# Making the fourth layer's context keys and values in 24 units beside the first layer's chain

## The chip, the cores and the metric

One core of a Trainium2 chip runs one program. The metric is the device time of a run in microseconds. Three runs of the kernel before took 933.57, 928.25 and 932.36 us, median 932.36.

## What is computed

The reference is a four-layer stack of gated cross-attention and feed-forward blocks. `x` is 8 batches of 56 tokens, 128 wide; the context is 8 batches of 1500 rows, 128 wide. What matters here:

- Layer 0: attention to the context with normalised, positive key features, so that only sums over the context are needed (per batch a 128 x 128 matrix and a vector), then a feed-forward block with ternary weights and 8-bit activations.
- Layer 1: attention in a window over the first 56 context rows, then 16 experts.
- Layer 2: attention of latents to the layer-normed context. The keys' L2 norms over 8 heads of 64 are needed for every context row.
- Layer 3: attention of 16 heads to all 1500 context rows with keys `ctx @ Wk.T` and values `ctx @ Wv.T`, then 8 experts. The keys are needed as a 16-bit part and a 16-bit remainder.

What depends on the context alone can be made before `x` is known: layer 0's sums, layer 2's normed context and key norms, layer 3's keys and values.

## The kernel before, in words

Five engines run programs of their own, written out by hand and joined by semaphores; each runs its instructions strictly in the order written. SyncE (`sync`) issues all DMAs, also in order: a wait there holds back every later DMA.

**The context pass** (about 9 to 252 us) is one turn per batch b, with buffers p = b % 2. TensorE's `context` makes, from the turned context `cT[p]`: the centred context (L679, three banks "D", PSUM 3 to 5), layer 3's keys (L687, three uses of banks D), layer 0's keys and values (L696, six uses of banks "A", PSUM 0 to 2), `l0_sums` of the batch before (L658, banks 6 and 7), layer 3's values (L708, three uses of banks A), half of `l2_keys` of the batch before (L668, twelve 125 x 512 products in all, 16-bit), the transposes of the normed context (L721) and the other half. VectorE scales the centred context (L1698), takes the keys' remainders `k_lo` (an L1519 with a 16-bit result), makes `kpr` (L1664), the statistics of the next batch (L1678 on `c_in`), reduces the squares (L1717), makes `kn` (L1519, 125 x 1536), and sums the squares of `l2_keys` (`l2_norms`, L1670) around the remainder of `clnT`. ScalarE copies and squares (L1190 `k_hi`, L1196, L1198, L1211 and L1213 the values into `v3`, L1181 squares, L1222). GpSimd waits for `kn`, applies gain and bias (L1411, L1412) and makes `rhs0` from `c_in` (L1420), which ends the use of `c_in[p]`.

`bank_a` and `bank_d` are the cyclic uses of three banks each; `a_uses` counts those of A. In `store_results` SyncE stores per turn `cln`, three copies of the keys (`k_hi`, `k_lo`, `k_hi`, L489), the values (L491), loads `cT` and, after `l0_rhs`, `c_in` of batch b + 2 (L453), and stores `clnT`. Weights come in portions after turns 1 to 5, the broadcast `vec` with turn 3.

**After the pass** come the key norms of the last batch (12 tiles), then the chain of layer 0: a layernorm of `x` (each with a 4-element power on GpSimd, L1430), the products of L738 and L742 and the queries, the attention result `at0` (signalled by `l0_att`, VectorE after L785), its store to `d_att` and load back as `y2` (L530, L533), `quantised_weights` on VectorE (L1619 to L1626), the dense product, a layernorm and the first feed-forward block (`quantised_ffn`, eight hidden products into eight banks). Layer 1 follows: queries, `key_blocks` on GpSimd (L1444), `scores1`, and `shift1` on VectorE, whose first mask addition (L1519 into 128 x 1024) starts at 345 us. Beside the chain SyncE loads layer 1's and 2's weights and the first experts into `wex`.

Of the kernel before, what the change touches and what calls it, by code (L numbers as in the profile page):

```python
# [15 lines left out]
D = 128  # L16
# [99 lines left out]

PRODUCT = {"latent_q": 18, "latent_k": 22, "latent_qT": 23, "queries2": 24}
# [57 lines left out]

def a_uses(b):

    return 0 if isinstance(b, int) and b == 0 else 21 * b - 12


def build(nc, io, out):
    ctx = ExitStack()
    with ctx:
# [86 lines left out]
        clnT = [carve([D, 2, C], F16) for _ in range(2)]  # L270
# [5 lines left out]
        k_hi = [carve([D, C], F16) for _ in range(2)]  # L276
        k_lo = [carve([D, C], F16) for _ in range(2)]
        v3 = [carve([KP, KT, 192]) for _ in range(2)]
        sqk = carve([KP, SQ, I2])
        stat = carve([KP, KT, 6])  # L280
        sm = carve([KP, 16, 24])
        wraw = carve([D, 5, FF])
# [101 lines left out]
        w_ready = sem("weights_ready")  # L384
        c_var, c_sd = sem("context_variance"), sem("context_deviation")
# [64 lines left out]
        def _(sp):  # L450
# [31 lines left out]
            def store_results(b, p, more=True):  # L482

                sp.wait_ge(d_free, 9 * b + 3 + 3)
                sp.dma_start(batch(d_cln, b), cln[p].rearrange("p j d -> p (j d)")).then_inc(st[p], 16)

                sp.wait_ge(d_free, 9 * b + 3 + 6)
# [8 lines left out]
                sp.wait_ge(d_free, 9 * b + 3 + 9)  # L496
                sp.dma_start(batch(d_clnT, b), clnT[p]).then_inc(st[p], 16)

            portions = {1: rest[0:1], 2: rest[1:2], 3: rest[2:5], 4: rest[5:10], 5: rest[10:14]}
            for b in range(B):  # L500
                store_results(b, b % 2, more=b + 2 < B)
                for dst, src in portions.get(b, ()):
                    sp.dma_start(dst, src).then_inc(ld_w, 16)

            for p in range(2):
                sp.wait_ge(st[p], 96 * (B // 2 + 1))
# [11 lines left out]
            for dst, name in ((w_kT2, "L2_wkT"), (w_vT2, "L2_wvT"), (w_o2, "L2_wo"), (w_q2, "L2_wq"),  # L518
                              (qk_col, "qk_cols")):
                sp.dma_start(dst, io[name]).then_inc(ld_m, 16)  # L520

            def load_experts1(g, p):
                sp.dma_start(wex[p][:, 0:G1 * 3 * D], batch(io["L1_ex"], g)).then_inc(ex_ld[p], 16)

            load_experts1(0, 0)
            load_experts1(1, 1)


# [5 lines left out]
                .then_inc(l0_ld, 16)  # L534

# [48 lines left out]
            sp.wait_ge(l3_free, 1)  # L584
            for p in range(2):
# [39 lines left out]
        def _(pe):  # L625
# [21 lines left out]
            def bank_d(b, n):  # L647

                pe.wait_ge(d_free, 9 * b + n + 1)
                return 3 + n % 3  # L650

            def l0_sums(b, p):
# [3 lines left out]
                pe.wait_ge(acc_used, b + 1)  # L656
                for j in range(KT):
# [4 lines left out]
            def l2_keys(turn, p, first_use, tiles=range(KT)):  # L662

                pe.wait_ge(d_free, 9 * turn + 3)
                for j in tiles:
                    k = bank_a(turn, first_use + j)
# [5 lines left out]
            def context(b, p, loads, first=False):  # L672
# [12 lines left out]
                for u in range(3):  # L685
                    k = bank_d(b, 3 + u)
                    pe.matmul(ps[0:D, k, 0:4 * KP], w_k3,  # L687
                              cT[p][:, 4 * u:4 * u + 4, :].rearrange("p j n -> p (j n)"),
                              start=True, stop=True).then_inc(d_full, 1)

# [1530 lines left out]
```

## Time and profile before

| | |
|---|---|
| median of three runs | 932.36 us |
| the profiled execution's own time | 930.32 us |
| its span | 928.7 us |
| busy TensorE, VectorE, ScalarE, GpSimd | 743.2, 632.5, 397.1, 277.1 us |
| mean granted clock of TensorE | 0.861 of full |
| bytes moved by DMA | 93.98 MB, 101 GB/s over the span |
| context pass, to the memset ahead of the first layernorm | 253 us |
| from there to the first mask addition of layer 1 | 92 us |

The profile gives for one execution when each instruction began and how long it took, what ended the idle time ahead of it, and for a stretch the busy time of each engine, the clock granted to TensorE (1.00 is 2.4 GHz, 0.50 is 1.2 GHz), the busy share of the 16 DMA engines and what they moved. Instructions that begin one after another on one engine overlap a little, so a row's mean can exceed the distance to the next. A line such as L1519 is that of a helper and stands for many operations; they are told apart by shape.

### The profile page before, as it was taken

The page shows a single profiled execution, that of the slowest core. Times are in us where ns is not written, and L with a number is a line of the kernel's source. Part 1 is how long each engine was busy: PE and PEld are TensorE (multiplying, and loading weights), DVE is VectorE, ACT ScalarE, POOL GpSimd, SP SyncE. Part 2 cuts the span into 40 slices and gives each one's busy share as a digit, 9 for nine tenths or more (in the row PEclk, how much of TensorE's full clock was granted, in tenths as well). Part 3 has the DMA queues.
Part 4 walks back from the last instruction along what each step waited for, and adds up shares of the span by engine and source line. Part 5 has one row for each costly group of instructions (what it writes and reads, how often), then busy time and mean ns, then how long its engine had stood idle before and what let it go on. Part 6 is the DMA issues. An engine that isn't in the chain of part 4 may idle for free.

```text
span 928.7 us, 16098 instructions
## 1 busy us (share of the span) xinstructions
PE 743.2 (80%) x5460; PEld 491.3 (53%) x5460; DVE 632.5 (68%) x1302; ACT 397.1 (43%) x650; POOL 277.1 (30%) x215
## 2 busy tenths in 40 slices
PE   4879998899744357698589999993479999985996
PEld 3757776677532224566245555552226656653665
DVE  4879988897768847355655566557587998915653
ACT  1556656566500203154344544541006766752441
POOL 1441234423213011045147777770050000000111
PEclk9889999999965557599799999997558998996999
DMA  6467666564232000011502242205703445500230
GB/s 188 156 214 262 247 205 227 181 214 149 76 103 20 0 0 1 1 51 52 154 5 69 76 128 72 69 1 76 156 1 103 130 128 151 164 2 23 69 102 21
DMA packets 46648, 93.98 MB, mean 101 GB/s; under 512 B 16698, under 2 KB 30010, under 8 KB 44274
## 3 DMA queue, kind: packets, MB, share of 16 engines
q1 hardware_dynamic: 46594, 93.25, 34.5%
q8 instruction: 35, 0.57, 0.3%
q14 instruction: 19, 0.16, 0.1%
HBM read 61.58 MB, written 31.65 MB: 100 GB/s over the span
## 4 chain that ended last, share of the span: by engine, by line
PE 38%; DVE 23%; issue 4%; ACT 3%; POOL 3%; DVEq 0%; POOLq 0%; ACTq 0%
DVE arena L2067 8%; PE ps L972 7%; PE ps L962 6%; DVE arena L1519 5%; PE ps L907 3%; PE ps L1132 2%; PE ps L1142 2%; PE ps L1070 2%; PE ps L1059 2%; ACT arena L1350 1%; POOL arena L1489 1%; PE ps L920 1%; PE ps L1044 1%; PE ps L841 1%; POOL arena L1430 1%
## 5 line engine op out<-in xcount | busy, mean ns | idle before, releaser
L1519 DVE TENSOR_TENSOR arena<-ps,arena 128x448 f32<-128x448 f32 (+8 forms) x160 | 99.4, 642 | 66.8 <-ACT arena L1373 20.5
L2067 DVE TENSOR_REDUCE arena<-ps 112x1 f32<-112x500 f32 x192 | 115.5, 669 | 17.9 <-PE ps L1044 17.0
L1489 POOL TENSOR_TENSOR arena<-arena 125x448 f32<-125x448 f32 x96 | 108.8, 1133 | 24.5 <-ACT arena L1327 21.7
L1350 ACT ACTIVATE arena<-ps 125x896 f32<-125x896 f32 x96 | 87.0, 917 | 30.0 <-PE ps L1059 29.4
L1430 POOL TENSOR_TENSOR arena<-arena 112x4 f32<-112x4 f32 x11 | 11.3, 1024 | 292.8 <-DVE arena L1543 286.8
L972 PE MATMUL ps<-arena 125*128 125x448 f32 (+1 forms) x208 | 97.1, 548 | 1.3 <-ACT arena L1327 0.8
L1519 DVE TENSOR_TENSOR arena<-ps,rn 125x448 f32<-125x448 f32 x96 | 59.3, 618 | 50.0 <-PE ps L962 45.7
L1327 ACT ACTIVATE arena<-arena,kbias 125x448 f32<-125x448 f32 x96 | 63.7, 668 | 65.0 <-DVE arena L1519 46.3
L962 PE MATMUL ps<-arena 128*125 128x448 f16 (+3 forms) x312 | 78.0, 360 | 3.0 <-DVEq L1530 3.0
L668 PE MATMUL ps<-w_k2h,arena 128*125 128x512 f16 x288 | 69.0, 397 | 12.4 <-ACT arena L1213 12.2
L1411 POOL TENSOR_TENSOR arena<-arena,vec 125x1536 f32<-125x1536 f32 x8 | 27.6, 3455 | 152.9 <-DVE arena L1519 152.9
L962 PEld LDWEIGHTS ps<-arena 128*125 128x125 f16 (+1 forms) x312 | 40.8, 135 | 57.2 <-issue 42.3
L1670 DVE TENSOR_REDUCE rn<-arena 125x512 f32 (+1 forms) x96 | 60.9, 682 | 4.7 <-ACT arena L1181 4.7
L1181 ACT ACTIVATE arena<-ps 125x512 f32<-125x512 f32 x96 | 57.3, 597 | 15.4 <-PE ps L668 11.4
L1464 POOL TENSOR_TENSOR arena<-arena 112x512 f32<-112x512 f32 x26 | 32.9, 1266 | 99.8 <-DVE arena L1519 99.4
L1044 PE MATMUL ps<-arena 64*112 64x500 f16 x192 | 55.5, 452 | 7.1 <-issue 4.3
L668 PEld LDWEIGHTS ps<-w_k2h,arena 128*125 128x125 f16 x288 | 40.4, 143 | 36.4 <-ACT arena L1213 13.4
L1070 PE MATMUL ps<-arena 125*32 125x168 f32 x768 | 51.5, 342 | 8.4 <-ACT arena L1350 8.4
L972 PEld LDWEIGHTS ps<-arena 125*128 125x128 f32 (+1 forms) x208 | 37.8, 189 | 13.9 <-issue 8.4
L1132 PE MATMUL ps<-arena 128*128 128x448 f16 x192 | 41.4, 367 | 3.1 <-DVE arena L1519 3.0
L1059 PE MATMUL ps<-arena 64*125 64x112 f16 x768 | 43.8, 242 | 0.0
L696 PE MATMUL ps<-w_l,arena 128*125 128x256 f32 x192 | 43.0, 381 | 0.0
(276 smaller groups left out, 1361.9 us busy)
## 6 DMA issues: line engine op xcount, KB each, us to landing
d_k<-arena SPq DMA_DIRECT2D x24, 375.0 KB
d_v<-arena SPq DMA_DIRECT2D x8, 1125.0 KB
arena<-d_k SPq DMA_DIRECT2D x96, 93.8 KB
arena<-d_v SPq DMA_DIRECT2D x8, 1008.0 KB
arena<-in_ctxT SPq DMA_DIRECT2D x8, 750.0 KB, 13.6
d_cln<-arena SPq DMA_DIRECT2D x8, 750.0 KB
d_clnT<-arena SPq DMA_DIRECT2D x8, 750.0 KB
arena<-d_clnT SPq DMA_DIRECT2D x8, 750.0 KB
```

The costliest lines, as they stand in the source:

```text
L668: mm = pe.matmul(ps[0:KP, k, :], clnT[p][:, a, KP * j:KP * j + KP], w_k2h[:, w, :], start=(n == 0), stop=(n == 2))
L962: mm = pe.matmul(ps[0:rows, (t + p) % 2, 0:N].rearrange("p (h q) -> p h q", h=H8), clnT_s[p][:, a, cols:cols + rows], qtT[:, q, :, bass.ds ...
L972: pe.matmul(ps[0:D, 4 + 2 * p, 0:N], cln_s[p][0:rows, t, :], pexp[(t + p) % 2][0:rows], start=(t == 0), stop=(t == KT)).then_inc(l2_pv, 1)
L1044: pe.matmul(ps[0:TT, max_bank(bn, u), 0:500], q.rearrange("p o h q -> p (o h q)"), kst[pn][64 * r:64 * r + 64, g, 500 * third:500 * third ...
L1059: mm = pe.matmul(ps[0:KP, 2 * (t % 2) + r, 112 * g:112 * g + 112], kst[p][rows, g, KP * t:KP * t + KP], qst3[rows, b:b + 1, g, 2 * r:2 * r ...
L1070: pe.matmul(ps[32 * g:32 * g + 32, 6, 0:168], v3s[p][:, t, 32 * g:32 * g + 32], p3[t % 2][:, 3 * g:3 * g + 3, :].rearrange("p h q -> p (h ...
L1327: act.activation(pexp[(t + p) % 2][0:rows], sscl[(t + p) % 2][0:rows], ACT.Exp, bias=bias)\
L1350: act.activation(p3[t % 2].rearrange("p (k h) q -> p k (h q)", k=2), ps[0:KP, 2 * (t % 2):2 * (t % 2) + 2, 0:8 * S], ACT.Exp).then_inc(l3_ ...
L1489: ins = pool.tensor_tensor(psum2[p][0:rows], psum2[p][0:rows], pexp[(t + p) % 2][0:rows], ALU.add)
L1519: return dve.tensor_tensor(out, a, b, op)
L1670: dve.tensor_reduce(rn[:, bass.ds(turn - 1, 1), j, :].rearrange("p o h -> p (o h)"), sqk[:, j % SQ, :].rearrange("p (h d) -> p h d", h=H8) ...
L2067: dve.tensor_reduce(mx3[bn % 2][:, u % 2, u % 8 // 2, u // 8:u // 8 + 1], ps[0:TT, max_bank_of(bn, u), 0:500], AX.X, ALU.max).then_inc(l3_ ...
```

## The change

Layer 3's keys and values leave the context pass and are made in 24 units of a third of a batch (500 columns). A unit is one 128 x 500 key product into bank 6 and four 125 x 128 value products into bank 7 (TensorE, `later`), two copies of the keys (16-bit and 32-bit) and two of the values (ScalarE, `later`), the key remainder (GpSimd, `remainders`), and four stores (SyncE, `store_later`). Its results lie in two sets of buffers, `late_hi`, `late_k`, `late_lo`, `late_v`, by the unit's parity; ScalarE waits with unit u until the four stores of unit u - 2 have landed (`st_l`). Units 0 to 2 are batch 0 and run in its turn; 3 to 8 are batches 7 and 6, whose `cT` is still there; the others read `cT` reloaded into `wex` (`load_later`). The units stand at fixed places of each program, in groups.

The key norms of the last batch move from the end of the pass to behind `l0_att`, in banks 3 to 5. `quantised_weights` moves from VectorE to GpSimd; VectorE keeps the scales. The load of `cT` in `store_results` waits for the `w_l0` products. The first feed-forward block uses six banks for its hidden products, and both blocks two in place of four for the turned hidden tiles. Layer 2's weights and the first experts are loaded later, and SyncE and VectorE wait for all 24 units, VectorE ahead of `shift1(0)`.

```diff
@@ store_results, SyncE
-                for s, part in enumerate((k_hi[p], k_lo[p], k_hi[p])):
-                    sp.dma_start(k3_in[bass.ds(b, 1), s].rearrange("o h d c -> (o h) d c"), part).then_inc(st[p], 16)
-                sp.wait_ge(a_free, a_uses(b) + 3 + 9)
-                sp.dma_start(batch(d_v3, b), v3[p].rearrange("p j d -> p (j d)")).then_inc(st[p], 16)
+                if b == 0:
+                    for u in range(3):
+                        store_later(u)
                 if more:
+                    sp.wait_ge(a_full, a_uses(b) + 6)
                     load_turned(b + 2, p)
                     sp.wait_ge(l0_rhs, b + 1)
                     load_context(b + 2, p)
...
+            def load_later(i):
+                sp.dma_start(wex[i % 2][:, 0:C], io["ctxT"][LATER[3 + i]]).then_inc(ld_x[i % 2], 16)
+
+            def store_later(u):
+                b, at, h = LATER[u // 3], 500 * (u % 3), u % 2
+                sp.wait_ge(l_lo, u + 1)
+                for n, part in enumerate((late_hi[h], late_lo[h], late_hi[h])):
+                    sp.dma_start(k3_in[b:b + 1, n, :, :, at:at + 500].rearrange("o h d c -> (o h) d c"), part)\
+                        .then_inc(st_l[h], 16)
+                sp.wait_ge(lv_taken, u + 1)
+                sp.dma_start(batch(d_v3, b)[:, 768 * (u % 3):768 * (u % 3) + 768],
+                             late_v[h].rearrange("p j d -> p (j d)")).then_inc(st_l[h], 16)
...
+            for u in range(3, 9):
+                store_later(u)
 
             sp.wait_ge(l0_att, 1)
...
+            for u in range(9, 24):
+                store_later(u)
+                if u in (11, 14, 17):
+                    sp.wait_ge(lv_full, u + 1)
+                    load_later(u // 3 - 1)
...
@@ TensorE
+            def later(*units):
+                for u in units:
+                    i, third = u // 3 - 3, u % 3
...
+                    if u:
+                        pe.wait_ge(lk_taken, u)
+                    pe.matmul(ps[0:D, 6, 0:4 * KP], w_k3, tiles.rearrange("p j n -> p (j n)"),
+                              start=True, stop=True).then_inc(lk_full, 1)
+                    if u:
+                        pe.wait_ge(lv_taken, u)
+                    for j in range(4):
+                        mm = pe.matmul(ps[0:KP, 7, D * j:D * j + D], tiles[:, j, :], w_v3, start=True, stop=True)
+                    mm.then_inc(lv_full, 1)
...
-                for u in range(3):
-                    k = bank_d(b, 3 + u)
-                    pe.matmul(ps[0:D, k, 0:4 * KP], w_k3,
...
-            l2_keys(B, 1, 0)
...
+            later(3, 4)
+            later(5, 6)
+            later(7, 8)
...
+            later(9, 10)
+            pe.wait_ge(l0_att, 1)
+            l2_keys(B, 1, 0, bank=3)
+            pe.wait_ge(a_free, a_uses(B) + 3 + KT)
             pe.wait_ge(l0_ld, 16)
             transposes(y2, 4)
+            later(11)
...
+            later(12, 13, 14, 15, 16)
+                    later(17, 18)
+            later(19, 20, 21)
@@ ScalarE
+            def later(*units):
+                for u in units:
+                    h = u % 2
+                    if u >= 2:
+                        act.wait_ge(st_l[h], 64 * (u // 2))
+                    act.wait_ge(lk_full, u + 1)
+                    act.copy(late_hi[h], ps[0:D, 6, 0:500])
+                    act.copy(late_k[h], ps[0:D, 6, 0:500]).then_inc(lk_taken, 1)
+                    act.wait_ge(lv_full, u + 1)
...
+            later(7, 8, 9, 10)
+            l2_squares(B, 0, bank=3)
+            later(11)
...
+            later(12, 13, 14, 15, 16)
             for t in range(NT):
                 act.wait_ge(h_in[0], t + 1)
...
+            later(17, 18, 19, 20, 21, 22, 23)
@@ GpSimd
+            def remainders(*units):
+                for u in units:
+                    pool.wait_ge(lk_taken, u + 1)
+                    pool.tensor_tensor(late_lo[u % 2], late_k[u % 2], late_hi[u % 2], ALU.subtract).then_inc(l_lo, 1)
...
+            remainders(9, 10)
+            quantised_weights()
+            remainders(11)
+            rsqrt()
+            remainders(12)
+            rsqrt()
+            remainders(13, 14, 15, 16)
             pool.wait_ge(l1_k, 1)
             key_blocks(0)
+            remainders(17, 18)
             key_blocks(1)
+            remainders(19)
             rsqrt()
+            remainders(20, 21, 22, 23)
@@ VectorE
-            quantised_weights()
+            weight_scales()
+            l2_norms(B, 0)
...
+            for p in range(2):
+                dve.wait_ge(st_l[p], 64 * 12)
             shift1(0)
```

## Rows read from the trace of the kernel before

**Rows 1.** Windows: us, busy us and count of each engine, clock, DMA share, GB/s.

```profile
96.00:120.00 24.00, 23.32 (x141) 18.35 (x140) 22.21 (x54) 15.26 (x35) 7.66 (x5) 1.00 0.75 265
...
288.00:312.00 24.00, 6.84 (x48) 4.41 (x48) 20.03 (x51) 2.52 (x3) 7.36 (x5) 0.50 0.15 15
```

**Rows 2.** Timeline of VectorE in the pass: start us, duration us, instruction.

```profile
32.83 1.75 DVE L1519 TENSOR_TENSOR arena<-arena 125x1536 f32<-125x1536 f32 x1
...
87.05 1.75 DVE L1519 TENSOR_TENSOR arena<-arena 125x1536 f32<-125x1536 f32 x1
...
113.29 1.75 DVE L1519 TENSOR_TENSOR arena<-arena 125x1536 f32<-125x1536 f32 x1
...
127.88 0.67 DVE L1519 TENSOR_TENSOR arena<-ps,arena 128x500 f16<-128x500 f32 x1
...
130.36 0.95 DVE L1664 TENSOR_SCALAR arena<-arena 125x1536 f32<-125x1536 f32 x1
134.63 2.42 DVE L1678 BATCH_NORM_STATS2 arena<-arena 125x6 f32<-125x128 f32 x12 [3.32 <-DMA arena<-in_ctx]
...
142.33 1.75 DVE L1519 TENSOR_TENSOR arena<-arena 125x1536 f32<-125x1536 f32 x1
...
226.20 1.75 DVE L1519 TENSOR_TENSOR arena<-arena 125x1536 f32<-125x1536 f32 x1
...
243.12 0.29 DVE L1659 COPY kv_all<-ps 128x130 f32<-128x130 f32 x1 [4.33 <-PE ps L658]
```

**Rows 3.** Timeline of VectorE and SyncE behind the pass.

```profile
253.21 0.09 DVE L1760 MEMSET arena<- 128x32 f32 x1
...
284.54 0.34 SPq L530 DMA_DIRECT2D d_att<-arena  x1
...
286.58 7.58 DVE L1622 TENSOR_SCALAR arena<-arena,wscale 128x512 f32<-128x512 f32 x5
...
291.92 0.33 SPq L533 DMA_DIRECT2D arena<-d_att  x1
...
345.03 1.23 DVE L1519 TENSOR_TENSOR arena<-ps,cst 128x1024 f32<-128x1024 f32 x1 [3.80 <-PE ps L841]
```

**Rows 4.** Timeline of TensorE in the pass, the moved products.

```profile
125.95 3.17 PE L687 MATMUL ps<-arena,w_k 128*128 128x500 f32 x6 [0.76 <-DVE arena L1698]
...
136.82 2.78 PE L708 MATMUL ps<-w_v,arena 128*125 128x128 f32 x24
```

**Rows 5.** Instructions by line and shape: busy us, mean ns, idle before.

```profile
L1190 ACT CAST arena<-ps 128x500 f16<-128x500 f32 x24 | 13.8, 575 | 38.8 <-PE ps L687 38.8
...
L1211 ACT COPY arena<-ps 125x384 f32<-125x384 f32 x24 | 11.7, 489 | 0.0
...
L1464 POOL TENSOR_TENSOR arena<-arena 112x512 f32<-112x512 f32 x26 | 32.9, 1266 | 99.8 <-DVE arena L1519 99.4 <-POOL arena L1464 0.4
...
L1433 POOL MEMSET arena<- 128x1152 f32 x1 | 1.1, 1057 | 0.0
```

**Rows 6.** Timeline, the first reload of the context and its reader.

```profile
44.63 0.33 SPq L453 DMA_DIRECT2D arena<-in_ctx  x1
...
50.58 2.42 DVE L1678 BATCH_NORM_STATS2 arena<-arena 125x6 f32<-125x128 f32 x12 [5.17 <-DMA arena<-in_ctx]
```

**Rows 7.** DMA issues: operation, count, KB each, median us to landing.

```profile
wex<-in_L_ex SPq DMA_DIRECT2D x6, 576.0 KB, 3.9
...
d_rl<-arena SPq DMA_DIRECT2D x1, 14.0 KB, 1.7
```

**Rows 8.** Timeline of SyncE's queue: issues in groups, us for the whole group.

```profile
104.13 1.83 SPq L489 DMA_DIRECT2D d_k<-arena  x3
...
217.16 3.88 SPq L489 DMA_DIRECT2D d_k<-arena  x3
...
636.17 4.94 SPq L576 DMA_DIRECT2D arena<-d_k  x12
```

**Rows 9.** Windows of one us while one value store is under way.

```profile
231.00:232.00 1.00, 1.00 (x10) 0.88 (x9) 1.00 (x3) 1.00 (x4) 0.92 (x2) 1.00 0.33 138
```

More of the change, by code:

```diff
@@ L275, in build @@
         rhs0 = carve([KP, KT, D + 2])
[L276 to L279, printed above, removed]
         stat = carve([KP, KT, 6])
         sm = carve([KP, 16, 24])
+        at[0] = CTX_TOP
+        clnT0 = carve([D, 2, C], F16)
+        at[0] = LATE_AT
+        late_hi = [carve([D, 500], F16) for _ in range(2)]
+        late_lo = [carve([D, 500], F16) for _ in range(2)]
+        late_k = [carve([D, 500]) for _ in range(2)]
+        late_v = [carve([KP, 4, 192]) for _ in range(2)]
+        clnT = [clnT0, carve([D, 2, C], F16)]
+        at[0] = SQK_AT
+        sqk = carve([KP, SQ, I2])
+        at[0] = 32520
         wraw = carve([D, 5, FF])
@@ L384, in build @@
         w_ready = sem("weights_ready")
+        lk_full, lk_taken = sem("later_keys_full"), sem("later_keys_taken")
+        lv_full, lv_taken = sem("later_values_full"), sem("later_values_taken")
+        l_lo = sem("later_keys_remainders")
+        h_used = sem("first_hidden_banks_used")
+        w_scales = sem("weight_scales_ready")
+        ld_x = [sem(f"later_context_loaded{i}") for i in range(2)]
+        st_l = [sem(f"later_results_stored{i}") for i in range(2)]
         c_var, c_sd = sem("context_variance"), sem("context_deviation")
@@ L660, in l0_sums, with l2_keys @@
                 mm.then_inc(acc_full, 1)
-            def l2_keys(turn, p, first_use, tiles=range(KT)):
-                pe.wait_ge(d_free, 9 * turn + 3)
+            def l2_keys(turn, p, first_use, tiles=range(KT), bank=0):
+                pe.wait_ge(d_free, 6 * turn + 3)
                 for j in tiles:
-                    k = bank_a(turn, first_use + j)
+                    k = bank + bank_a(turn, first_use + j)
                     for n, (a, w) in enumerate(((0, 0), (0, 1), (1, 0))):
@@ L703, in context @@
                     l0_sums(b - 1, 1 - p)
-                for u in range(3):
-                    k = bank_a(b, 6 + u)
-                    for j in range(4):
-                        mm = pe.matmul(ps[0:KP, k, D * j:D * j + D], cT[p][:, 4 * u + j, :], w_v3,
-                                       start=True, stop=True)
-                    mm.then_inc(a_full, 1)
+                if first:
+                    later(0, 1, 2)
                 if first:
@@ L1185, in context @@
                     deviation(0)
-                act.wait_ge(st[p], 96 * loads)
-                for u in range(3):
-                    act.wait_ge(d_full, 9 * b + 3 + u + 1)
-                    act.copy(k_hi[p][:, 500 * u:500 * u + 500], ps[0:D, 3 + u, 0:500]).then_inc(k_hi_ready, 1)
                 act.wait_ge(l0_kn, b + 1)
@@ L1432, in _ @@
             rsqrt()
+            remainders(3, 4)
             ch.link(pool.memset(v1, 0.0))
@@ L1437, in _ @@
             pool.nop().then_inc(l1_zero, 1)
+            remainders(5, 6)
             rsqrt()
+            remainders(7, 8)
             def key_blocks(i):
@@ L1730, in context @@
                 if not first:
-                    l2_norms(b, 9, range(KT // 2))
+                    l2_norms(b, 6, range(KT // 2))
                 for u in range(3):
@@ L1874, in normalise1 @@
                 ins.then_inc(l1_on, 1)
+            for p in range(2):
+                dve.wait_ge(st_l[p], 64 * 12)
             shift1(0)
```

166 lines of the change are left out of this document (91 added, 75 removed).

## The prediction, made before the change was built

> **What bounds the kernel now.** I read the windows first, to see which stretch is full of what [rows 1]. Between 96 and 120 us TensorE is busy for 23.3 of 24 us and VectorE for 22.2: the context pass is short of engine time. Between 288 and 312 TensorE is busy for 6.8 us, at half clock, and ScalarE for 2.5: the first layer is a chain of small dependent steps, with room beside it. The change moves work from the first stretch to the second, and the question is what limits each afterwards.
>
> Next, the period of the pass. I mark a turn by T, the start of VectorE's multiply of 125x1536 that makes `kn` [rows 2]. T goes from 32.83 (batch 0) to 226.20 (batch 7), so seven turns take 193.4 us. An undisturbed one takes 26.2 (87.05 to 113.29), the next 29.0 (113.29 to 142.33) because the statistics wait 3.32 us for `in_ctx`. That wait closes a loop beside the engines: `kn` goes to GpSimd, whose three passes free `c_in`; only then is the next context load issued, 11.8 us after T (32.83 to 44.63 for batch 0 [rows 2, 6]); it lands after L; and from the start of the statistics to the next T there are 7.7 us (134.63 to 142.33). A turn can't be shorter than 19.5 + L.
>
> Third, the chain that follows it, from VectorE's memset at 253.21 to VectorE's first mask addition on the second layer's scores at 345.03 [rows 3]: 91.8 us, with the first layer's attention ready (`l0_att`) at 284.5, as the store of `d_att` shows.
>
> **The context pass.** Removed per turn: TensorE's 3.17 (keys) and 2.79 us (values) [rows 4]; VectorE's three remainders, 127.88 to 130.36, 2.5 us [rows 2]; ScalarE's 3 x 0.58 + 3 x 0.78 = 4.1 us [rows 5], the 0.78 being a 0.49 copy and its 128-wide sister of 0.29; 2250 KB of stores. VectorE's own path would then be 14.6 (T to the end of the norms and `cln`, 113.29 to 127.88), 0.95 for the key features and 7.7, so 23.2 us. But the loop is longer: L was 5.95 us where I can read it (issue 44.63, statistics 50.58) [rows 6], with the end of a value store still under way; the expert load of 576 KB lands in 3.9 us [rows 7], which in proportion is 5 for these 750 KB. I take L = 5.5 and 25.0 us a turn, bounds 24.4 and 25.5. So of about 3 us of VectorE work a turn only 1.2 come through.
>
> The start loses something. T of batch 0 comes at about 27.4 instead of 32.8, but units 0, 1 and 2 follow there with two buffers. Unit 0 is taken at 26.3, its remainder ends at 28.8, its stores are issued until 31 and land at 35.4; only then is unit 2 taken, and its remainder holds GpSimd until 37.9. GpSimd's passes (10.1 us) end at 48.0 against 44.6 before, and T of batch 1 is 48.0 + 5.5 + 7.7 = 61.2 (58.28 before). Then two turns of 25.0; one of 29.0, since the load of batch 5 will meet the broadcast of `vec` as before; two of 25.5; the last, which loads nothing, waits for ScalarE's squares: these end where TensorE's `w_l0` products end, 3.4 us earlier than in the 25.9 us of before, 22.5. T of batch 7: 61.2 + 50 + 29 + 51 + 22.5 = 213.7, so 12.5 us earlier. The last key norms leave the tail: from T to the memset were 27.0 us (226.20 to 253.21), and 17.2 (to the end of the copy at 243.12) remain [rows 2, 3]: 9.8 more. Together **22.3 us gained**, bounds 15 (L = 6 to 9) and 29.
>
> **The chain.** A unit costs TensorE 3.17/3 + 2.79/3 = 2.0 us at 2.4 GHz, 4.0 at 1.2; ScalarE 0.58 + 0.57 + 0.49 + 0.29, pipelined 1.7; GpSimd 1.3 for the remainder (112x512 takes 1.27) [rows 5]; SyncE four issues. Up to `l0_att` units 3 to 8 stand in front of three chain products of TensorE. Its idle stretches there are 5.0, 4.0 and 3.6 us, a pair of units takes 4.0 (at half clock 8), so I add 2 us, bounds 0 and 12.
>
> Then the stores set the pace. ScalarE may take unit u only when the four stores of unit u-2 have landed. One such period is: 1.15 (two copies), 1.3 (remainder), three key stores issued, 0.3 (value store issued), its landing, 0.4 for semaphores. An issue of a key store took 1.83/3 = 0.61 at best and 3.88/3 = 1.3 at worst as a mean of three [rows 8]; a load with runs of 1000 bytes took 0.41 (4.94/12). The new ones have a third of the bytes; I take 0.55, bounds 0.36 and 1.24. The value store has 125 rows of 3 KB, 384 KB. Such stores ran at a DMA share of 0.29 to 0.35 and 101 to 138 GB/s (228 to 234 us, with one value store in flight; one of these six windows is in [rows 9]): 2.8 us of transfer, and 1.7 for a store of hardly any bytes, `d_rl` [rows 7], so 4.5 us. The period is 1.15 + 1.3 + 1.65 + 0.3 + 4.5 + 0.4 = 9.3 us, **4.65 a unit**.
>
> The Trainium skill (DMA: Bandwidth & Descriptors, Anatomy of one DMA) prices a DMA of its software path at about 2.0 us plus bytes over 436 GB/s. By it this store would land in 2.9 us instead of 4.5, the period would be 7.7 and the sum 922; the row of the share speaks for the other value.
>
> The queue of SyncE matters too. It waits for `l0_att`, stores `d_att`, stays blocked until that has landed (284.54 to 291.92, 7.4 us) and issues the load; unit 9's stores stand behind it. So unit 11 is taken at `l0_att` + 7.4 + 0.3 + 2.0 + 4.5 + 0.7 = 14.9. Units 11, 13, ... 23 share a buffer: seven periods later, 65.1, the last store lands, and VectorE waits for it before the first mask addition. Between units 16 and 17 ScalarE has a table load and four Silus and GpSimd key blocks of 3.5 us: 4 more. That is `l0_att` + 84, where 345.03 - 284.5 = 60.5 was enough: **23.5 us lost**.
>
> Costed at nothing: the weights' quantisation (VectorE 286.58 to 297.2 before [rows 3]), now on GpSimd. Its price there lies between 0.92 ns an element (memset of 1152 in 1.06) and 2.5 (a two-operand pass of 512 in 1.27) [rows 5], for 3 x 2560 elements 7 to 19 us; the cover is the 16 us until unit 12's remainder, and at the upper end some 3 us come through. VectorE gets 12 norms, 7.8 us, instead; with TensorE's 12 tiles they end about where `d_att` arrives (294.66), so the removal of 10.6 us from VectorE gains little: `xT2` at 297.12 could have come no earlier than 295.7. Reloading ScalarE's table for the square root (1.3) is beside the chain. If the unit line were fast, these would be next.
>
> **The sum.** -22.3 + 2 + 23.5 = +3.2. The profiled execution took 930.3 us (span 928.7), so 933.5; the median of the runs shown is 2 us above it and the lowest 2 below, so I say 934.
>
> **Rivals.** *Stores are quicker (faster).* If a value store uses all DMA engines, it lands like the loads do, 3.9 for 576 KB and so about 3.2 for 375; with issues of 0.4 the period is 7.6, seven save 12 us: 922, and 919 with L = 5. For it: short issues were seen for 1000-byte runs. Against it: the share of a third in [rows 9], which a smaller store of the same 125 rows doesn't change. Chance 0.30. The Trainium skill's rule above, from the same page, points the same way.
>
> *SyncE is held by the key stores (slower).* Place: the three key issues in the store of each unit. If each holds SyncE for 1.24, the median before, the period is 11.3; seven add 14 us, unit 9's own issue 2 more: 950. It decides from about 0.75 us an issue. For it: six of the eight triples before took over 3 us, some in a nearly empty queue. Against: one took 1.83, and bytes are a third. Chance 0.20.
>
> *TensorE stays at 1.2 GHz in the chain.* The stretch 288 to 312 shows a granted clock of 0.50, 1.2 GHz, at 6.8 us of work [rows 1]. Units then take 4.0 us of it and TensorE, not the stores, sets the pace; 12 tiles cost 8 more: +20 to +30, 955 to 960. Against: the units themselves fill it. Chance 0.07.
>
> *The pass hardly shortens.* The change moves its work, but the load loop holds each turn at 19.5 + L with L at 7 to 9 us, since stores of `clnT` and `cln` follow each load: the pass gives 6 instead of 12.5 and the end is 940. Chance 0.08.
>
> *Forecast*, 0.35: within 928 to 940.
>
> **The numbers.** What a measurement tells from no change is 0.5%, 4.7 us: 927.7 to 937.0. Faster: the first rival and a sliver of the forecast, 0.31. Same: most of the forecast, 0.28. Slower: the rest, 0.41. The range reaches from the first rival to the second with margins: 916 to 955; the forecast's own is 928 to 940.
>
> **What would show it.** In the profile of after: turns of 25 us whose statistics wait for `in_ctx`; the memset at 231 instead of 253; ScalarE's copies of odd units 9 us apart, each idle until a DMA; VectorE's first mask addition waiting some 8 us for a value store, near 350. The forecast is wrong if value stores land in under 3.5 us, if key store issues hold SyncE for 0.36 or 1.2 us, if ScalarE waits for TensorE instead of stores in the chain, or if turns come at 23 us (L under 4).

## The result, and the profile after

The changed kernel takes **967.3 us** (median of 4 runs, 965.8 to 968.9), the kernel before 932.1 beside it: a ratio of 1.0385, 95% interval 1.0349 to 1.0421. It is slower by 35 us, where I had forecast 934, and the time lies above my range of 916 to 955. An execution that took over 1.5% longer than the fastest of its kernel is left out of the comparisons below.

| us | before | after | forecast |
|---|---|---|---|
| T of batch 7 | 226.2 | 214.6 | 213.7 |
| VectorE's memset, end of the pass | 253.2 | 232.9 | 230.9 |
| from there to `l0_att` | 31.3 | 36.8 | 33.3 |
| from `l0_att` to the first mask addition | 60.5 | 114.1 | 84 |
| from there to the end of the span | 583.7 | 581.2 | 583.7 |
| span | 928.7 | 964.9 | 931.9 |

Read `l0_att` as the issue of the `d_att` store in before and as the end of VectorE's last multiply in front of it, 269.65, in after. The pass is what I forecast; the loss is in the fourth line of the table. In the profile's page, of after, the chain that ended last has DMA at 8%, which the same line of before doesn't list:

```profile
PE 38%; DVE 20%; issue 15%; POOL 10%; DMA 8%; ACT 5%; SPq 3%; POOLq 0%; DVEq 0%; ACTq 0%
```

and ScalarE stood idle for 100.0 us in front of the first copies of the units, 77.9 of them for a value store (columns as in [rows 5]; this group answers to its first row, where the wait was 38.8 us, for TensorE):

```profile
L1256 ACT CAST arena<-ps 128x500 f16<-128x500 f32 x24 | 13.8, 575 | 100.0 <-DMA d_v<-arena 77.9
```

Timeline of VectorE, of after: four of its lines, the answer to [rows 2, 3].

```profile
84.86 2.42 DVE L1779 BATCH_NORM_STATS2 arena<-arena 125x6 f32<-125x128 f32 x12 [2.18 <-DMA arena<-in_ctx]
92.57 1.75 DVE L1626 TENSOR_TENSOR arena<-arena 125x1536 f32<-125x1536 f32 x1
...
117.85 1.75 DVE L1626 TENSOR_TENSOR arena<-arena 125x1536 f32<-125x1536 f32 x1
...
232.89 0.09 DVE L1853 MEMSET arena<- 128x32 f32 x1 [0.36 <-DVE kv_all L1760]
...
383.73 1.23 DVE L1626 TENSOR_TENSOR arena<-ps,cst 128x1024 f32<-128x1024 f32 x1 [16.11 <-DMA d_v<-arena]
```

A turn is 25.3 us (92.57 to 117.85) and its statistics wait for the context load, as forecast; the memset comes at 232.89; and the first mask addition stands 16.11 us for a value store. Timelines of SyncE and of ScalarE, of after, in the first part of the chain:

```profile
237.02 1.85 SPq L526 DMA_DIRECT2D d_k<-arena  x3
238.91 0.50 SPq L529 DMA_DIRECT2D d_v<-arena  x1
239.47 4.24 SPq L526 DMA_DIRECT2D d_k<-arena  x3
243.75 0.51 SPq L529 DMA_DIRECT2D d_v<-arena  x1
248.45 1.83 SPq L526 DMA_DIRECT2D d_k<-arena  x3
250.33 0.50 SPq L529 DMA_DIRECT2D d_v<-arena  x1
...
269.68 0.33 SPq L557 DMA_DIRECT2D d_att<-arena  x1
280.72 0.33 SPq L560 DMA_DIRECT2D arena<-d_att  x1
```

```profile
246.22 0.58 ACT L1256 CAST arena<-ps 128x500 f16<-128x500 f32 x1 [3.92 <-DMA d_v<-arena]
...
250.77 0.58 ACT L1256 CAST arena<-ps 128x500 f16<-128x500 f32 x1 [2.94 <-DMA d_v<-arena]
...
256.95 0.58 ACT L1256 CAST arena<-ps 128x500 f16<-128x500 f32 x1 [3.68 <-DMA d_v<-arena]
```

Unit 3's value store is issued at 238.91 and releases unit 5 at 246.22: 7.3 us. The next two take 7.0 (243.75 to 250.77) and 6.6 (250.33 to 256.95); over all units whose store released ScalarE it is 6.1 to 10.2 us. The last one of all, issued at 375.93, releases the mask addition at 383.73, after 7.8. I had put 4.5 on it. SyncE's three key issues take 1.8 us in an idle queue (0.61 each, where I had 0.55), but 4.24 where they follow a value store directly. And the store of `d_att` takes 11.0 us to land, 269.68 to 280.72, where it took 7.4.

Windows of after, the answer to [rows 1]:

```profile
96.00:120.00 24.00, 21.28 (x120) 17.06 (x119) 21.49 (x53) 13.73 (x30) 8.58 (x6) 0.93 0.51 188
288.00:312.00 24.00, 11.51 (x82) 7.75 (x80) 15.01 (x45) 8.18 (x16) 13.38 (x7) 0.82 0.46 137
```

In the chain TensorE has 11.5 us of work instead of 6.8 and a granted clock of 0.82 instead of 0.50, so TensorE isn't held at half clock; the DMA share has gone from 0.15 to 0.46. Windows of one us, of after, across that third landing (columns as in [rows 9]):

```profile
250.00:251.00 1.00, 1.00 (x6) 1.00 (x6) 0.00 (x0) 0.23 (x1) 0.00 (x0) 0.50 0.72 208
251.00:252.00 1.00, 1.00 (x5) 0.77 (x4) 0.32 (x1) 1.00 (x3) 0.10 (x1) 0.53 0.65 174
252.00:253.00 1.00, 1.00 (x4) 0.52 (x3) 0.97 (x4) 0.75 (x3) 0.97 (x1) 1.00 0.33 68
253.00:254.00 1.00, 1.00 (x9) 0.77 (x8) 0.93 (x8) 0.27 (x1) 0.03 (x1) 1.00 0.30 74
```

For two us after the value store's issue the share is 0.72 and 0.65, which I take for the three key stores, issued in the 1.8 us before it. Only then does the value store show alone, at a share of a third, and at 68 and 74 GB/s, not at the 101 to 138 that I had read around [rows 9].

### The profile page after: what moved, and what is told of

Same layout as the page of the kernel before. It is cut to its first block, busy times and chain, and to the rows that moved or that the text cites. A ratio compares the mean times of both kernels' runs of the same rounds, so it can differ in the third digit from the quotient of the medians.

```text
span 964.9 us, 16156 instructions
## 1 busy us (share of the span) xinstructions
PE 747.8 (78%) x5460; PEld 497.6 (52%) x5460; DVE 612.1 (63%) x1271; ACT 409.8 (42%) x675; POOL 321.7 (33%) x246
## 4 chain that ended last, share of the span: by engine, by line
PE 38%; DVE 20%; issue 15%; POOL 10%; DMA 8%; ACT 5%; SPq 3%; POOLq 0%; DVEq 0%; ACTq 0%
DVE arena L2168 8%; PE ps L1046 7%; DMA d_v<-arena 6%; PE ps L1036 6%; DVE arena L1626 4%; PE ps L981 3%; PE ps L1206 2%; PE ps L1216 2%; SPq L526 2%; POOL arena L1498 2%; PE ps L1144 2%; POOL arena L1507 2%; PE ps L1133 1%; ACT arena L1431 1%; POOL arena L1596 1%
## 5 line engine op out<-in xcount | busy, mean ns | idle before, releaser
L1626 DVE TENSOR_TENSOR arena<-ps,arena 128x448 f32<-128x448 f32 (+8 forms) x136 | 83.1, 635 | 72.5 <-ACT arena L1369 20.5
L736 PE MATMUL ps<-w_k2h,arena 128*125 128x512 f16 x288 | 78.0, 428 | 29.8 <-ACT arena L1270 29.8
L736 PEld LDWEIGHTS ps<-w_k2h,arena 128*125 128x125 f16 x288 | 42.9, 153 | 58.1 <-ACT arena L1270 34.0
L1489 POOL TENSOR_TENSOR arena<-arena 128x500 f16<-128x500 f32 x24 | 27.7, 1154 | 112.7 <-ACT arena L1257 112.7
L1144 PE MATMUL ps<-arena 125*32 125x168 f32 x768 | 49.5, 328 | 9.7 <-ACT arena L1431 8.4
L1256 ACT CAST arena<-ps 128x500 f16<-128x500 f32 x24 | 13.8, 575 | 100.0 <-DMA d_v<-arena 77.9
```

Of the source, the lines that this page charges most:

```text
L736: mm = pe.matmul(ps[0:KP, k, :], clnT[p][:, a, KP * j:KP * j + KP], w_k2h[:, w, :], start=(n == 0), stop=(n == 2))
L1144: pe.matmul(ps[32 * g:32 * g + 32, 6, 0:168], v3s[p][:, t, 32 * g:32 * g + 32], p3[t % 2][:, 3 * g:3 * g + 3, :].rearrange("p h q -> p (h ...
L1626: return dve.tensor_tensor(out, a, b, op)
```

## The experiments

All kernels ran beside the kernel before. Its median was 930.8 us in the first series of four, 931.1 in the second and 931.6 in the third. Several medians below carry a spread of about 1%. Much of it goes with the clock: the same stretch of the kernel, from the load of the fourth layer's padding to the end of the span, took 298.7 us in the two profiles with a mean granted clock of 0.82 in it, 294.9 to 295.2 in the four with 0.83, 290.9 to 292.7 in the five with 0.84, and 289.6, 292.6 and 295.4 in the three with 0.85. So I compare times by their intervals, and stages by marks inside the profile.

### Four sets of unit buffers

```diff
+        late_hi.append(carve([D, 500], F16))
+        late_lo.append(carve([D, 500], F16))
+        late_v += [carve([KP, 4, 192]) for _ in range(2)]
...
-                b, at, h = LATER[u // 3], 500 * (u % 3), u % 2
+                b, at, h = LATER[u // 3], 500 * (u % 3), u % 4
...
-                    if u >= 2:
-                        act.wait_ge(st_l[h], 64 * (u // 2))
+                    if u >= 4:
+                        act.wait_ge(st_l[h], 64 * (u // 4))
+                    if u >= 2:
+                        act.wait_ge(l_lo, u - 1)
```

> The changed kernel (967.3 us) with four sets of unit buffers instead of two; all work and all stores stay. Theory S (the ring of stores sets the pace: ScalarE may take unit u only when the stores of unit u-2 have landed, and a value store lands 7.4 us after its issue, not 4.5): with four sets a period of about 13.4 us covers four units instead of two, so the ring no longer binds; VectorE's 16.1 us wait for d_v before the first mask addition falls to under 5 us, ScalarE's waits for d_v go, and the time falls to 925-942 us. Rival W (the copies, products and remainders themselves hold the chain): the wait only moves, 958-967 us. Rival D (the transfers share one limit, so that more of them in flight land later): landings rise from 7.4 to over 11 us and the time is 948-960 us.

Measured: 937.5 and 944.9 us, some 26 less than the changed kernel (and 954.2 and 957.4). Two times are too few to choose between the ranges of the theories, so the profile must. In it ScalarE never waits for a store any more, and yet the first mask addition waits longer, 18.95 us. Timelines of SyncE and VectorE, with four sets:

```profile
338.56 3.79 SPq L535 DMA_DIRECT2D d_k<-arena  x3
342.39 0.63 SPq L538 DMA_DIRECT2D d_v<-arena  x1
343.07 4.05 SPq L535 DMA_DIRECT2D d_k<-arena  x3
347.16 0.48 SPq L538 DMA_DIRECT2D d_v<-arena  x1
347.69 4.01 SPq L535 DMA_DIRECT2D d_k<-arena  x3
351.75 0.48 SPq L538 DMA_DIRECT2D d_v<-arena  x1
```

```profile
360.83 1.22 DVE L1637 TENSOR_TENSOR arena<-ps,cst 128x1024 f32<-128x1024 f32 x1 [18.95 <-DMA d_v<-arena]
```

The units are ready early, and now SyncE is the queue: a unit every 4.6 us (338.56, 343.07, 347.69), nearly all of it key issues that take 4 us instead of 1.8, and the last value store lands after 9.1 (351.75 to 360.83). So the ring of two buffers was only half of it. Behind it stood the stores themselves, as the third of the three theories had it, though with a landing of 9, not 11.

### The value store as two stores, 112 and 13 rows

```diff
-                sp.dma_start(batch(d_v3, b)[:, 768 * (u % 3):768 * (u % 3) + 768],
-                             late_v[h].rearrange("p j d -> p (j d)")).then_inc(st_l[h], 16)
+                dst, src = batch(d_v3, b)[:, 768 * (u % 3):768 * (u % 3) + 768], late_v[h].rearrange(...)
+                sp.dma_start(dst[0:112], src[0:112]).then_inc(st_l[h], 16)
+                sp.dma_start(dst[112:KP], src[112:KP]).then_inc(st_l[h], 16)
```

> The changed kernel with each unit's value store of 125 rows issued as two, 112 and 13 rows, like the loads of the context. Theory S with its part on the number of DMA engines (125 rows are served by five of sixteen): from the issue to the point at which ScalarE takes unit u+2 is 4.0-5.5 us instead of 7.4, each of seven periods is 2-3 us shorter, l0_att comes 3 us earlier: 943-953 us. Rival (the landing is long because of the three key stores ahead of it and the latency of a write, whatever the number of engines): it stays at 6.5-7.5 us and the extra issue of 0.5 us a unit gives 966-972 us.

Measured: **931.2 us**, 0.9992 of the kernel before (0.9957 to 1.0027). This one edit, which adds 24 DMA issues and moves the same bytes, takes back all that the change had lost. It went further than the theory said. Timelines of SyncE and of ScalarE, of this kernel:

```profile
235.49 1.90 SPq L526 DMA_DIRECT2D d_k<-arena  x3
237.44 0.58 SPq L530 DMA_DIRECT2D d_v<-arena  x1
238.06 0.43 SPq L531 DMA_DIRECT2D d_v<-arena  x1
240.61 1.84 SPq L526 DMA_DIRECT2D d_k<-arena  x3
242.50 0.60 SPq L530 DMA_DIRECT2D d_v<-arena  x1
243.14 0.42 SPq L531 DMA_DIRECT2D d_v<-arena  x1
...
257.93 0.33 SPq L558 DMA_DIRECT2D d_att<-arena  x1
265.42 0.33 SPq L561 DMA_DIRECT2D arena<-d_att  x1
```

```profile
240.91 0.57 ACT L1257 CAST arena<-ps 128x500 f16<-128x500 f32 x1 [1.15 <-DMA d_v<-arena]
...
245.87 0.58 ACT L1257 CAST arena<-ps 128x500 f16<-128x500 f32 x1 [0.53 <-DMA d_v<-arena]
```

and one window across the landing of unit 8's value stores, issued from 253.44 to 254.50 with no other issue before 257.93:

```profile
255.00:256.00 1.00, 1.00 (x5) 0.54 (x5) 0.90 (x4) 0.04 (x1) 0.00 (x0) 1.00 0.81 255
```

With wide stores the landing is 3.5 us from the first of the two issues (237.44 to 240.91; 242.50 to 245.87 is 3.4), half of the 7. The share is 0.81 and the rate 255 GB/s where it had fallen to 0.3 and 70. Every triple of key issues is back at 1.8 to 2.0, and `d_att` at 7.5 (257.93 to 265.42). Three terms that I had taken for separate (landing, key issues, `d_att`) came back together, with one edit, so they had one cause. I read it so: a store of 125 rows keeps a few DMA engines long, and whatever else goes through those engines waits with it. The profile shows the share of all engines and not which ones were busy.

The share of a third was the sign of it. 125 is 5 x 25, and five of sixteen engines are 0.31, the share in [rows 9] and in the windows above. The Trainium skill says this (DMA: Bandwidth & Descriptors, Why a DMA increments its semaphore by 16 and not by 1): a DMA is spread over the largest number of engines up to 16 that divides the slowest dimension of both its sides. The trace agrees: with 112 rows, which 16 divides, the share was 0.81. No run splits the rows in another way that leaves both parts narrow; that the row count counts, and not that there are two stores, rests on the shares, and on the key stores, single ones of 128 rows, at up to 0.72 in the same trace as the 0.33. The Trainium skill's price from the prediction (DMA: Bandwidth & Descriptors, Anatomy of one DMA), by which such a store lands in an estimated 2.9 us, is stated for its software path; it is near the 3.4 of the wide store here and far from the 7 of the narrow one.

### The two halves of the change alone, on the kernel before

Key remainders from VectorE to GpSimd, still in the pass:

```diff
+                    act.copy(k_full[:, 500 * u:500 * u + 500], ps[0:D, 3 + u, 0:500]).then_inc(k_hi_ready, 1)
...
-                    tt(k_lo[p][:, 500 * u:500 * u + 500], ps[0:D, 3 + u, 0:500],
-                       k_hi[p][:, 500 * u:500 * u + 500], ALU.subtract).then_inc(d_free, 1)
...
+                        pool.tensor_tensor(k_lo[p][:, cols], k_full[:, cols], k_hi[p][:, cols], ALU.subtract)\
+                            .then_inc(k_lo_ready, 1)
```

> The kernel before (932.1 us), with keys and values of the fourth layer left in the context pass, but the three key remainders of a batch taken from VectorE (2.5 us a turn) and given to GpSimd behind its pass over the context (about 3.3 us a turn of 13 idle ones), from a second copy by ScalarE; the key and value stores are issued behind the next context load. Theory P (TensorE, 25.5 of 26.2 us of a turn in the kernel before, holds the pass once VectorE is relieved): turns fall from 27.6 on the mean to about 26, 918-926 us. Rival V (VectorE alone held it): turns of 24-25, 908-916 us. Rival L (the load's loop of GpSimd's pass and landing holds it): turns as before, 929-935 us.

Measured: 932.0 us, 1.0031 (1.0002 to 1.0059). Rival L holds: VectorE has 2.5 us less to do per turn, and its statistics wait for the load instead, 1.5 to 8.2 us. Timeline of VectorE, of this kernel:

```profile
107.79 2.42 DVE L1691 BATCH_NORM_STATS2 arena<-arena 125x6 f32<-125x128 f32 x12 [5.21 <-DMA arena<-in_ctx]
...
115.48 1.75 DVE L1532 TENSOR_TENSOR arena<-arena 125x1536 f32<-125x1536 f32 x1
...
144.28 1.75 DVE L1532 TENSOR_TENSOR arena<-arena 125x1536 f32<-125x1536 f32 x1
```

The last batch's key norms moved behind `l0_att`, with the quantisation on GpSimd:

```diff
-            l2_norms(B, 0)
             dve.wait_ge(acc_used, B + 2)
...
-            quantised_weights()
+            weight_scales()
+            l2_norms(B, 0)
```

> The kernel before with only the other half of the change: the last batch's twelve key norms moved from the end of the context pass to behind l0_att, and the weights' quantisation from VectorE to GpSimd; no unit of keys and values moved. Theory N (the end of the pass loses 9.8 us, and with no unit stores the chain has room for the norms, so at most 3 come back): 922-926 us. Rival (the norms, 7.8 us of VectorE and 12 tiles of TensorE at half clock, and GpSimd's 19 us of quantising push the layer norm behind the feed-forward by 6-10 us): 929-934 us.

Measured: 930.2 us, 0.9987 (0.9965 to 1.0010). The end of the pass comes 7.7 us earlier (memset at 245.50), and all of it is given back: the first mask addition is at 346.88, against 345.03 before. Timeline of VectorE, of this kernel:

```profile
288.17 3.73 DVE L1804 TENSOR_SCALAR rn<-rn 125x768 f32<-125x768 f32 x1
...
304.24 6.88 DVE L1571 TENSOR_SCALAR arena<-x,arena 112x128 f32<-112x128 f32 x4 [1.13 <-POOL arena L1436]
```

The second line is four small scalings that took 1.12 us in the kernel before. Here GpSimd makes its key blocks at the same moment (6.86 us from 304.17), because its quantisation has kept it busy until 298.4, and VectorE is held until it is done: 5.8 us lost in one place. In the kernel before, GpSimd had made them long since. The clamp of the norms takes 3.73 us beside the quantisation, against 0.56 in the kernel before. That kernel had such a meeting of its own: its five scalings of the quantisation took 7.58 us from 286.58 [rows 3], beside 7.16 us of GpSimd's key blocks from 286.31. So my "beside other work, at nothing" was wrong for the quantisation on GpSimd even with no unit stores about.

### Wide stores everywhere

Four kernels with the split of 112 and 13 rows for `d_cln` in the pass as well, and for `d_v3` wherever it is stored:

```diff
-                sp.dma_start(batch(d_cln, b), cln[p].rearrange("p j d -> p (j d)")).then_inc(st[p], 16)
+                dst, src = batch(d_cln, b), cln[p].rearrange("p j d -> p (j d)")
+                sp.dma_start(dst[0:112], src[0:112]).then_inc(st[p], 16)
+                sp.dma_start(dst[112:KP], src[112:KP]).then_inc(st[p], 16)
```

On the changed kernel:

> The changed kernel with the value stores of the units split into 112 and 13 rows (931.2 us by itself) and the store of d_cln (125 rows of 6 KB) of each context turn split the same way. If narrow stores in the pass also lengthen the landing of the context load behind them (5.2-5.8 us), it falls to about 4.5 and each of five turns is 0.7-1.3 us shorter: 924-928 us. Rival: the load then meets d_cln on all engines instead of on five, the landing stays or grows, and the time is 930-935 us.

Measured: 932.4 us, 1.0037 (1.0005 to 1.0069): the rival, no gain over the split of the unit stores alone. On the kernel before:

> The kernel before with its stores of d_v3 and d_cln (125 rows each) split into 112 and 13 rows: the baseline against which the change should be read once stores are wide. If the stores did no harm in the pass, whose turns wait for them only through the context load (0 to 4.7 us a turn): 922-930 us. If they don't matter there at all: 929-934 us. The change with split unit stores is at 931.2; so the change itself is worth between +9 and -3 us on this baseline.

Measured: 924.5 us, 0.9942 (0.9903 to 0.9981). Run again:

> The kernel before with wide stores of d_v3 and d_cln once more, beside the next three, since its first median (924.5 us) stood 9.7 us above the span of its own profile (914.8) and the others' did not: 916-924 us.

Measured: 922.9 us, 0.9915 (0.9884 to 0.9946). Timeline of VectorE, of the kernel before with wide stores (first profile):

```profile
113.61 1.75 DVE L1523 TENSOR_TENSOR arena<-arena 125x1536 f32<-125x1536 f32 x1
...
139.95 1.75 DVE L1523 TENSOR_TENSOR arena<-arena 125x1536 f32<-125x1536 f32 x1
...
166.18 1.75 DVE L1523 TENSOR_TENSOR arena<-arena 125x1536 f32<-125x1536 f32 x1
...
246.53 0.09 DVE L1764 MEMSET arena<- 128x32 f32 x1
```

The turns of 29.0 and 30.3 us of before (the first of them in [rows 2]) are gone: 26.3 and 26.2, with no wait for `in_ctx`. I had put that long turn down to the broadcast of `vec`. The loads of the weights are unchanged here; the narrow stores in front of the context load made it. A narrow `d_cln` alone doesn't make it: the changed kernel has one, with neither value nor key stores behind its first turn in the pass, and no long turn.

With four sets on the changed kernel:

> Four sets of unit buffers and all stores split. With landings of about 3 us, only 1 to 4 us of ScalarE's wait per unit is left for more buffers to remove; VectorE still waited 9.2 us for the last value store in the kernel with split stores. Theory S: that wait falls to under 4 us and the time is 918-926 us. Rival W (units now stand where TensorE reaches them in its order, and the last seven come after the first hidden product whatever the buffers): within 3 us of the kernel with two sets, 924-932 us.

Measured: 921.6 us, 0.9925 (0.9888 to 0.9962). The first mask addition is at 336.66, but it still waits 8.49 us, since units 19 to 23 are stored 3 us apart, one behind the other, in SyncE's queue. So the time is in the range of theory S, and its wait of under 4 us is not there. With remainders on GpSimd in the pass of the kernel before, twice:

> The kernel before with key remainders on GpSimd in the pass (931.9 us, its statistics waiting 1.5-8.2 us a turn for the context load) and d_v3 and d_cln stores split. If the narrow stores are what the load waits behind, turns fall from 27.7 to about 26, TensorE's own 25.5: 916-924 us. If not: 929-934 us.

> The same plus the key remainders on GpSimd in the pass (916.0 us before). In the profiles both passes end at the same point (memset at 246.5 and 247.5 us), TensorE holding either; so the theory that TensorE bounds the pass once stores are wide expects no difference between the two, within 3 us. If VectorE's 2.5 us a turn mattered, this one is 5-10 us faster.

Measured: 916.0 us, 0.9875 (0.9807 to 0.9943, 4 runs), and 920.1, 0.9901 (0.9868 to 0.9934, 12 runs). The second run, beside the same kernel without the remainders (922.9), is within 3 us of it, so relieving VectorE gave nothing that I can tell apart. TensorE is busy for 23.33 of 24 us (96 to 120) in the profile of either, which agrees with the theory that it holds both.

### Late norms without the collisions

The two collisions found above are taken out: GpSimd waits for the first hidden product before its key blocks, and the clamp comes behind the quantisation of `z`.

```diff
+            pool.wait_ge(h_in[0], 1)
             pool.wait_ge(l1_k, 1)
             key_blocks(0)
...
             quantise(z, y, zq, ((2, 0), (3, 1)))
+            dve.tensor_scalar(rn_flat, rn_flat, 1e-24, None, ALU.max).then_inc(rn_sq, 1)
```

> The kernel before with wide stores and the last key norms moved into the chain, with what cost the 7.7 us again in the kernel with late norms (930.2 us) put elsewhere: GpSimd's key blocks, beside which VectorE's scalings of z took 6.9 us instead of 1.1, only after the first hidden product, and the clamp of the norms (3.7 us beside the quantisation) behind the quantisation of z. Theory N2 (the two collisions between GpSimd and VectorE gave the gain back): 5-8 us below the kernel before with wide stores. Rival (the twelve tiles and the longer queue of VectorE in front of xT2 gave it back): 0-2 us below.

Measured, with wide stores: **916.9 us** (6 runs), 0.9845 (0.9801 to 0.9888), 6 us below the kernel with wide stores alone beside it (12 runs, 0.9915). The intervals overlap by a little (0.9884 to 0.9888), and a part of the 6 us goes with the clock: of the twelve runs six had a mean granted clock of 0.858 to 0.860 and took 924.2 to 929.1 us, and none of the six runs here was below 0.865. At 0.865 both kernels took 921.6, at 0.869 the one without late norms 918.7 to 920.2, and this one 917.5 at 0.866 and 916.3 and 918.0 at 0.870. In the profile both collisions are gone: the scalings of `z` take 1.11 us and the clamp 0.55. The chain from memset to mask addition grew from 91.7 us to 95.8, not to the 101.4 of the kernel with late norms and collisions, while the memset came 7.9 us earlier; so 3.7 us are left at the mask addition. So the collisions were worth 5.6 us of the chain, in the main as the theory has it, and the rival has a part too: 4.1 us are still given back. With all three together:

> All three together: wide stores, key remainders on GpSimd, late norms without the collisions. Theory: 5-8 us below the kernel with wide stores and remainders in the pass (about 908-911 us); rival: within 2 us of it.

Measured: 919.3 us, 0.9894 (0.9850 to 0.9937): the rival. Its pass ended with a wait of 5.43 us for `d_clnT`, a store that stands behind the key stores there. So the lowest ratio here is that of the kernel before with wide stores and late norms, 1.5% below the kernel before and 5% below the changed one; its interval overlaps those of the kernels with wide stores and the key remainders on GpSimd.

## Why the prediction was wrong

By its own steps, against after's profile. My sum was +3.2, the spans differ by +36.2, and the missing 33.0 are:

- **The pass and its tail: right.** -20.3 for -22.3. Turns of 24.7 to 25.3 for 25.0, statistics waiting for the load, L of 5.2 to 5.8 us for 5.5. Two errors cancelled: the first turn took 38.8 us instead of 33.8, because the narrow unit stores held SyncE and the context load (with wide unit stores it took 33.5), and the turn of 29.0 that I expected from `vec` didn't come. 2.0 us of the miss.
- **The chain to `l0_att`: +5.5 for +2.** I counted TensorE's products there and no store. But units 5 to 9 each stood 2.5 to 4.8 us for the value store of the unit two before, and TensorE's next chain product stands behind them. With wide stores this stretch is 29.5 us, shorter than before's 31.3. 3.5 us of the miss.
- **The unit line: the step that failed.** "So 4.5 us" for the value store's landing measured 6.1 to 8.4 in the first part of the chain and 6.4 to 10.2 behind `l0_att`. The step took transfer plus landing of a lone store. It left out that the keys of the same unit are still in transfer (2 us, share 0.7), and it took the rate of 101 to 138 GB/s from windows of before, where this one showed 68 and 74 once the keys were out (the last one of all did reach 95 to 137, after 4 us behind other transfers at shares of 0.75 to 1.0). Seven periods took 93.9 us (289.79 to 383.73) for 69.1 with my 4 for the Silus, 24.8 us of the miss, and not all of it is landing. The last three, where only stores hold the line, took 10.9, 10.5 and 12.8 us instead of 9.3: 6.3 us. The second took 14.3 (landing 10.2, with the second layer's weights being loaded behind the store): 5.0. The first took 17.1: 7.8, of which some 3 are landing and some 5 the quantisation on GpSimd, below. The third and fourth, with the Silus, took 13.7 and 14.7: 5.7 beyond my 4. In the third unit 16 waited for unit 14's value store, which took 10.2. In the fourth it is TensorE, not a store: unit 19's product stands in its order behind the second product of the feed-forward, and ScalarE stood 9.25 us for it. I had named such a wait as a sign that the forecast is wrong. Timelines of GpSimd and of ScalarE, of after:

```profile
289.38 6.85 POOL L1548 TENSOR_SCALAR wquant<-arena 128x2560 bf16<-128x2560 f32 x1
296.20 1.15 POOL L1489 TENSOR_TENSOR arena<-arena 128x500 f16<-128x500 f32 x1
```

```profile
349.52 0.58 ACT L1256 CAST arena<-ps 128x500 f16<-128x500 f32 x1 [9.25 <-PE ps L710]
```

- **The quantisation at nothing: wrong as well.** It took 19.2 us of GpSimd (276.98 to 296.2), my upper end, and began 7.3 us after `l0_att`, behind unit 10's remainder, which I had not counted. Unit 11's remainder, not unit 12's, is next in GpSimd's order. Its copies were out at 290.8 and it began at 296.20, so 5.4 us came through on the line that decides. With wide unit stores it was 7.6 (272.2 to 279.82).
- **`d_att`**: I let it take 7.4 us as before. Behind the unit stores it took 11.0, and with wide unit stores 7.5. With that and the longer landing of unit 9's value store, unit 11 is taken at `l0_att` + 20.1 instead of 14.9: 5.2 us of the miss. Behind the mask addition the profile of after is 2.5 us shorter. 2.0 + 3.5 + 24.8 + 5.2 - 2.5 = 33.0.
- **The rivals.** "Stores are quicker" gave 922 and priced a period at 7.6 us with two sets. Wide stores with two sets are what it describes: their last three periods took 7.6, 7.6 and 7.8 us, so the price was met, but the seven took 74.9, since the quantisation and TensorE's order hold the earlier ones, and the time was 931.2. That four sets gave 921.6 is luck. "SyncE is held by the key stores" was right on the place for some triples, but as a result of the same narrow stores, and not on top of a landing of 4.5; on the odd units' line only the last triple took longer (2.78 us). Its evidence was also misread: seven of the eight triples before took over 3 us, not six, and the worst was 4.55 (1.5 an issue), not 3.88. I treated the two as alternatives with one price each. They have one cause, so the high side of my range had to hold both, and it didn't.
- **The signs** I named were there: odd units' copies idle until a DMA, the mask addition waiting for a value store. I had it 8 us, at 350; it was 16.1, at 383.7.

Is the change itself bad? With the same wide stores on either side, the changed kernel stands at 932.4 with two sets and 921.6 with four, the kernel before at 922.9 to 924.5. With two sets, moving 24 units off the pass gains 19 us there (memset at 227.7 against 246.5) and gives all of it back in the chain; with four, whose interval overlaps that of the kernel before with wide stores, I can tell no gain. What stays open: which part of the chain's excess with wide stores and four sets (80.6 us from `l0_att` to the mask addition, against 60.5) is SyncE's queue, and which is TensorE's order; no run separates them. The trace shows both: ScalarE waits 11.05 us for unit 19's product, SyncE has nothing to issue from 310.0 to 318.3, and then the last five units go through it 3 us apart.

## What to carry to other kernels

When stores move to a place where something waits for them, read the DMA share of one while it is alone: a share of a third means that most engines are idle, and the price is not only its own transfer but every transfer and issue behind it. Split the rows so that sixteen divides them before judging such a change, and judge it against a baseline with the same split. Follow one moved unit through the written order of every engine that it passes, since whatever stands in front of it there (here the quantisation on GpSimd and the feed-forward on TensorE) adds to its line even where that engine is idle on the whole. Where two rivals make the same resource late, add them up for the edge of the range instead of choosing.

## What I had not expected of the hardware

- A narrow store slows what is issued behind it: three key issues took 1.8 us each time in the kernel with split unit stores, up to 2.0, and 4.2 (at 239.47) behind a narrow value store in the changed kernel. A long issue doesn't need a narrow store, though. In the pass of the kernel before, one issue of a narrow `d_cln` behind the loads of the weights held SyncE for 9.98 us, and with it all issues behind it; with wide stores it took 5.42. But in the changed kernel, where `d_cln` is narrow and neither value nor key stores are about, it took 5.50. So a narrow `d_cln` by itself doesn't give the 9.98. Timeline of SyncE, before, then of the kernel before with wide stores, then after:

```profile
129.12 9.98 SPq L485 DMA_DIRECT2D d_cln<-arena  x1
```

```profile
129.37 5.42 SPq L486 DMA_DIRECT2D d_cln<-arena  x1
```

```profile
133.62 5.50 SPq L507 DMA_DIRECT2D d_cln<-arena  x1
```

- GpSimd's two-operand passes held VectorE's scalings: 1.12 us became 6.88 beside 6.86 us of key blocks, so nearly the whole of GpSimd's run was waited out. With the key blocks moved away the same scalings took 1.11. Timeline of GpSimd, of the kernel with late norms:

```profile
304.17 6.86 POOL L1450 TENSOR_TENSOR arena<-arena,cst 128x896 f32<-128x896 f32 x4
```
